# Softmax sums of a causal attention block: the GpSimd adds key tiles 6 and 7 of the upper half too, with masks placed between its additions, and TensorE forms one product set of the sum

## What is computed

```python
scores = jnp.einsum('bhqd,bhkd->bhqk', q, k) / math.sqrt(hd)
scores = jnp.where(causal, scores, -jnp.inf)
att = jax.nn.softmax(scores, axis=-1)
out = jnp.einsum('bhqk,bhkd->bhqd', att, v)
```

## Time and profile before

| what | value |
|---|---|
| time, median of 3 runs | 2902.95 us (2901.94 to 2903.45) |
| the profiled execution | 2904.26 us, its span 2902.5 us |
| busy in the span: TensorE, VectorE, GpSimd, ScalarE | 96%, 55%, 44%, 37% |
| TensorE clock granted, mean | 0.98 |
| instructions | 41782 |

### The profile page before, as it was taken

How to read it: one execution, slowest core, us unless ns; L and a number is a source line. 1 busy time by engine, 2 the same in 40 slices (tenths; PEclk the granted TensorE clock), 3 DMA queues, 4 the chain that set the end, 5 groups by cost and what they waited for, 6 DMA issues and landing times. The chain is left out here.

```text
span 2902.5 us, 41782 instructions
## 1 busy us (share of the span) xinstructions
PE 2772.0 (96%) x16195; PEld 2009.4 (69%) x16195; DVE 1583.7 (55%) x3171; ACT 1060.7 (37%) x1449; POOL 1281.9 (44%) x671
## 2 busy tenths in 40 slices
PE   5999999999999999879999999999999978999997
PEld 3888888888888888745555555555555547888886
DVE  4232233222322122267777787888778746777775
ACT  1322222232213111146555566666655641112121
POOL 3322332233224211157777777777777761112120
PEclk8999999999999999979999999999999989999998
DMA  7544354545334644355555555555555545554541
GB/s 250 183 158 159 139 203 166 177 158 190 128 116 149 214 174 175 112 119 125 126 126 124 127 123 121 118 121 119 121 121 128 136 173 142 144 156 136 162 131 58
DMA packets 171709, 421.58 MB, mean 145 GB/s; under 512 B 22204, under 2 KB 74548, under 8 KB 170232
## 3 DMA queue, kind: packets, MB, share of 16 engines
q1 hardware_dynamic: 139240, 298.03, 30.3%
q10 hardware_dynamic: 32272, 120.88, 18.9%
HBM read 278.77 MB, written 139.56 MB: 144 GB/s over the span
## 5 line engine op out<-in xcount | busy, mean ns | idle before, releaser
L1185 ACT ACTIVATE prob<-ps_s 128x1024 f32<-128x1024 f32 (+3 forms) x768 | 597.6, 810 | 415.5 <-PE ps_s L1361 399.8
L846 PE MATMUL ps_u<-h_hi,w_hi 128*128 128x512 f32 x1536 | 612.3, 399 | 1.8 <-POOL h_lo L586 1.8
L846 PE MATMUL ps_u<-h_lo,w_hi 128*128 128x512 f32 x1536 | 600.8, 391 | 0.0
L846 PE MATMUL ps_u<-h_hi,w_lo 128*128 128x512 f32 x1536 | 599.7, 390 | 0.0
L1139 POOL TENSOR_TENSOR added<-added,prob 128x2048 f32<-128x2048 f32 (+1 forms) x128 | 551.5, 4308 | 4.6
L580 POOL TENSOR_TENSOR w_lo<-w_raw,w_hi 128x1024 fp32r<-128x1024 f32 x93 | 222.6, 2393 | 478.4 <-ACT w_hi L648 478.4
L719 DVE SCALAR_TENSOR_TENSOR qk_lo<-ps_u,bias_col,qk_hi 128x512 fp32r<-128x512 f32 x128 | 96.0, 750 | 578.7 <-ACT qk_hi L624 578.7
L1242 DVE TENSOR_REDUCE part_high<-ps_r 128x1 f32<-128x512 f32 x496 | 330.4, 685 | 91.0 <-PE ps_r L1331 90.6
L1238 DVE CUSTOM_DVE_ANT_0 ps_r<-ps_r,row_mask 128x384 f32<-128x384 f32 (+1 forms) x500 | 312.1, 630 | 105.4 <-PE ps_r L1331 104.7
L1331 PE MATMUL ps_r<-k_st,q_st 96*128 96x512 f32 (+1 forms) x1008 | 331.9, 387 | 23.0 <-DMA v_sb<-v_tok 9.5
L846 PEld LDWEIGHTS ps_u<-h_lo,w_hi 128*128 128x128 f32 x1536 | 288.6, 188 | 61.8
(11 more groups left out here) (192 smaller groups left out, 3437.0 us busy)
## 6 DMA issues: line engine op xcount, KB each, us to landing
w_raw<-w_cols SPq DMA_DIRECT2D x72, 512.0 KB, 6.3
qk_split<-qk_hi SPq DMA_DIRECT2D x64, 512.0 KB, 2.6
qk_split<-qk_lo SPq DMA_DIRECT2D x64, 512.0 KB, 4.0
q_st<-qk_split ACTq DMA_DIRECT2D x60, 512.0 KB, 7.5
k_st<-qk_split ACTq DMA_DIRECT2D x60, 512.0 KB, 13.7
xn<-in_L_attn_x SPq DMA_DIRECT2D x8, 2048.0 KB, 11.2
v_tok<-v_out SPq DMA_DIRECT2D x32, 512.0 KB, 4.4
wm<-in_L_wmod SPq DMA_DIRECT2D x8, 2048.0 KB, 8.9
```

The costliest lines, as they stand in the source:

```text
L846: last = nc.tensor.matmul(ps_u[u % 2][:], w[:, m, k], h[:, k, tok], start=k == 0 and j == 0, stop=k == KT - 1 and j == 2)
L1185: nc.scalar.activation(prob[:, buffer_of(t, k), 2 * pair:2 * pair + 2, off:], ps_s[pair][:, :, off:], ACT.Exp, scale=SCALE).then_inc(exp_d ...
```

## The change

GpSimd adds all the tiles of the upper half (7 additions); masks 9, 10 and 11 are placed behind additions 5, 6 and 7. TensorE's products with ones for steps 6 and 7 are gone in passes 0 to 30, and the product of `added` closes its bank. In the last pass (`LAST_ADDS` = 4) GpSimd stops after step 4, and TensorE takes the products of steps 5, 6 and 7.

```diff
-    ADDS = LONG - 3
+    ADDS = LONG - 1
+    LAST_ADDS = FIRST = LONG - CT
@@ GpSimd, one pass, behind add 4, mask 7, mask 8
-                if t < NG - 1:
-                    add(t, 5)
-                mask(t, 9)
-                mask(t, 10)
-                mask(t, 11)
-            add(NG - 1, 5)
+                for k in range(LAST_ADDS + 1, LONG):
+                    if t < NG - 1:
+                        add(t, k)
+                    mask(t, k + CT)
@@ TensorE, sum_high
-                pe.wait_ge(added_up, ADDS * (t + 1))
+                adds = ADDS if t < NG - 1 else LAST_ADDS
+                pe.wait_ge(added_up, ADDS * t + adds)
+                if adds < LONG - 1:
+                    pe.wait_ge(masked, masked_upto(t, LONG - 1))
                 for h in range(HG):
-                    nc.tensor.matmul(bank_of(use)[h * HD:(h + 1) * HD, :], ones[:], added[:, h], start=True, stop=False)
-                for k in range(ADDS + 1, LONG):
+                    last = nc.tensor.matmul(bank_of(use)[h * HD:(h + 1) * HD, :], ones[:], added[:, h], start=True, stop=adds == LONG - 1)
+                for k in range(adds + 1, LONG):
```

More of the change, by code:

```diff
@@ L938, in attend @@
     MASKS = QC * CT
-    FIRST = LONG - CT
     assert QC == 2 and steps[LONG][1] == 0 and steps[FIRST][1] == CT
```

## The result

The changed kernel takes 2929.09 us (median of 4 runs, 2927.74 to 2931.86), the kernel before beside it 2902.62: a ratio of 1.0090, 95% interval 1.0078 to 1.0102, so 26.5 us slower. The sign is as predicted, the size is three times the forecast of 8 us and above the range. The profiled execution took 2930.27 us, its span 2928.5 us (before: 2904.26 and 2902.5).

A forecast was written before the change was run, and what follows sets the result against it. TensorE was taken to set the pace, with VectorE last around `sum_high`. Full passes at +9.5 us and the last pass at -1.5 us gave +8.0 us, so 2911 us, range 2894 to 2918.

The forecast's parts named there:

- TensorE's gain: Around `sum_high`: of 0.77 us of removed matmuls a pass, only 0.30 us comes back, the rest becoming waits for banks.
- GpSimd's work and its place: In full passes: 3.6 us more GpSimd work a pass fits its idle time; add 7 covers the first low addition's start.
- The meeting: VectorE's first low addition waits for add 7, then precedes mask 11: 0.80 us late, about 0.40 us a typical pass.
- The rival with mask 11 in front: Mask 11 goes ahead of the waiting first low addition: 0.6 us more a pass, +25 us, 2928 us; chance 0.07.
- The first rival: The first low addition comes ahead of add 7: each pass gains 0.2 us, 8 us in all, 2895 us; chance 0.17.
- The last pass: End of `attend`: -3.2 us for add 5 gone, +1.25 for step 5's matmuls, +0.4 for a later add 1: -1.5 us.

The follow-up runs named there:

- the last pass alone: The kernel before with only the change's last pass: GpSimd drops add 5, TensorE takes the products of steps 5 to 7; 2898.57 us, ratio 0.9986.
- own wait: The changed kernel with GpSimd waiting for the end of its own mask 10 before it issues add 7; 2912.87 us, ratio 1.0047.

## Why the prediction went wrong

**TensorE's gain: right.** It said that only VectorE's 0.30 us of the 0.77 would come back. With the products left out alone it was 0.27 a pass, and in the changed kernel the removed time stands as waits for VectorE (0.57 us before 1793.80).

**GpSimd's work and its place: right.** Add 6 2.38 us (2.39), add 7 1.27 to 1.31 (1.30), LA1 up 0.33 us behind add 7's start (0.35).

**The meeting: the step that failed.** It said that LA1 "does its work only when that one has ended, and then goes ahead of GpSimd's next". The first half holds. The second was read from the earlier trace rows, where LA1 came up during mask 10 and got in ahead of mask 11, and the low addition of 512 columns during the last add 5, behind which GpSimd had nothing to do. Neither is the case of the change, an addition with a mask behind it: masks behind masks let LA1 in at that place in every kernel in which they met, and a last instruction can show nothing of what comes next. That it fails is seen in 3.15 us instead of 2.55, and the run with mask 11 held, where LA1 takes 2.56 us, shows what it cost: the 29 spacings are 14.2 us shorter. That this run's total, 2910.29 us, is also the forecast's 2911 is partly luck, for its last pass and `finish` differ as well. The rule of the Trainium skill that the prediction named (SBUF — State Buffer, "Who interferes with whom": they exclude each other, and who issues first has the shared pair for the whole instruction) agrees on the exclusion, 3.15 against 1.75 us. On who comes next, it gives the wrong winner if order of issue is read from the recorded starts: LA1's is 1787.86 and mask 11's 1788.77, and mask 11 went first. Whether mask 11 was issued before its recorded start no row shows.

**The arithmetic behind it: near, with luck in the total.** The rival with mask 11 in front reckoned 0.6 us more a pass and 2928 us; the kernel took 2929. It reckoned a typical pass 1.0 us longer, and 0.94 was measured by the medians, 0.85 on average; all its passes came to +26.9 us, and the measured ones, with what lies ahead of them, to +23.4. `finish`, 3.8 us longer in this trace and put at nothing in the prediction, makes up for that. The mistake was this rival's chance of 0.07. Two cases that differ in which of two waiting instructions goes next had stood at 0.48 and 0.07 on a single row. The first rival, reckoned at 2895, comes out at 2896.22 when it is made to happen.

**The last pass: two terms mis-sized, in opposite directions.** Up to LA1 of group 31 it said +0.4 and it was +3.5. Add 1 comes 6.55 us behind LA1 of group 30 instead of 5.54: 1.0 where 0.4 was reckoned, the same failed step once more. The other 2.5 us are the `v_sb` product's 11.09 us, which the earlier trace rows made me look for only behind the pass, not in it. From there to `finish` it said -3.2 + 1.25 = -1.95, and it was -4.7 (-4.55 with the last pass alone). The 3.2 held: TensorE's wait fell from 4.57 to 1.47 us in the run with the last pass alone. What was mis-sized is the price of the matmuls behind it: the 1.25 for step 5 was read from matmuls that ran at a lower clock (the windows above), and it was left out that a shorter wait makes the others faster too. In sum -1.2 against -1.5, near by luck.

**The range.** It ended at 2918 because it left out this rival. A rival which one row alone speaks against belongs inside it, though its price is 17 us above the likeliest.

## What to carry to other kernels

Where VectorE works on two SBUF operands, look in the timeline not only at whether GpSimd is busy then, but at what follows its running instruction without a pause: VectorE may wait for that too, or for a whole run of them (here 3.15 us for 1.75, and 11.09 for 1.55). Spare time as a sum (GpSimd had 205 us) says nothing of this; the place does. A wait that holds GpSimd's next instruction, or even one for its own last result, can be worth more than the work it delays, and moving less work (one addition instead of two, with mask 11 held) kept the gain without the meeting. One place in which VectorE got in, as in the earlier trace rows, is not enough to say that it will in another.

## What the runs showed of the hardware

- A waiting VectorE addition was passed over by GpSimd's next instruction: 3.15 us where waiting for the running one alone gives 2.56 (mask held) to 2.68 (own wait). In the last pass eight instructions passed by: 11.09 us, 2.17 with one wait; that moved the next low addition by 2.5 us. A wait that delays GpSimd by 0.1 us turned the order round in thirty of thirty passes.
- When VectorE got in first, GpSimd's additions paid instead (1.28 us became 2.60 and 2.80), and GpSimd had the time.
- A TensorE wait can cost more than itself, through the clock. Eight matmuls of 384 columns took 1.25 us start to start behind 4.57 us without work, at a granted clock of 0.59 over that stretch, and 0.64 us at a clock of 1.00 behind a wait of 1.47. In the changed kernel the last products with v, behind 4.37 us without work while VectorE's 11.09 us ran, were granted 0.50, the 1.2 GHz level:

```profile
2392.00:2397.00 5.00, 4.50 (x32) 1.38 (x32) 4.52 (x4) 0.29 (x2) 0.00 (x0) 0.50 0.14 52
```

It doesn't always follow: behind the same wait of 1.67 us in the last pass, TensorE was granted 1.00 in the changed kernel and 0.50 in the run whose last pass has the wait for the `v_sb` product (its product of `added` 1.07 and 1.94 us).
